# Layers 0 and 1 prepared two tiles ahead of the recurrent layer, a reordered start, and one order for the late iterations

## The reference

```python
# L0: per-sample scaled product, L1: tanh RNN, L2: per-sample rank-8 update of a base matrix, L3: LSTM
x = x + einsum('bsi,io->bso', x * ys[:, None, :], W0) * d[:, None, :]      # ys, d from cond
x = x + scan(h -> tanh(h @ Wh1 + (x_t @ Wx1 + b1)))                         # h0 = cond
x = x + x + x @ (base + A_b @ B_b)       # A_b, B_b = gelu(layernorm(cond) @ w1 + b1) @ w2 + b2
x = x + scan((h, c) -> LSTM(x_t @ Wx3 + b3 + h @ Wh3))                      # h0 = cond, c0 = 0
```

## Time and profile before

| what | value |
|---|---|
| time, median of 3 runs | 1170.16 us (1169.96 to 1170.26) |
| the profiled execution's own time | 1170.03 us |
| its span in the profile | 1168.2 us |
| TensorE busy | 1130.0 us, 97% of the span, 23548 matmuls |
| VectorE busy | 896.1 us, 77% |
| ScalarE busy | 424.4 us, 36% |
| mean granted TensorE clock | 0.994 of full speed |

### The profile page before, as it was taken

One profiled execution on the slowest core, in us unless ns is written; L12 is line 12 of the kernel. 1 busy time (PEld: TensorE's weight loads), 2 busy tenths in 40 slices (PEclk: granted clock), 3 DMA queues, 4 the chain that ended last, 5 costly groups with the idle time before them and its releaser, 6 DMA issues.

```text
span 1168.2 us, 52112 instructions
## 1 busy us (share of the span) xinstructions
PE 1130.0 (97%) x23548; PEld 773.1 (66%) x23548; DVE 896.1 (77%) x2656; ACT 424.4 (36%) x1036; POOL 53.5 (5%) x75
## 2 busy tenths in 40 slices
PE   5779999999999999999999999999999999999997
PEld 3446766776676677667667766766776676677586
DVE  7798777777777777787777778777777877777665
ACT  6784333333333333333333333333333333333322
POOL 0000100000000000000000000000000000000000
PEclk9989999999999999999999999999999999999999
DMA  9991000000000000000000000000000000000000
GB/s 339 404 349 29 21 21 21 3 21 21 21 20 21 21 3 21 21 21 21 20 21 4 21 20 21 21 21 21 3 21 20 21 21 20 12 3 12 12 13 21
DMA packets 24590, 51.08 MB, mean 44 GB/s; under 512 B 4160, under 2 KB 4288, under 8 KB 23344
## 3 DMA queue, kind: packets, MB, share of 16 engines
q1 hardware_dynamic: 24080, 47.56, 11.5%
q10 hardware_dynamic: 288, 0.20, 0.1%
HBM read 39.36 MB, written 8.39 MB: 41 GB/s over the span
## 4 chain that ended last, share of the span: by engine, by line
PE 92%; DMA 4%; SPq 2%; DVE 1%; ACT 1%; issue 0%; DVEq 0%; ACTq 0%
PE ps_gates L1488 55%; PE ps_l L1424 14%; PE ps_x L1424 7%; PE ps_rnn L1534 6%; PE ps_rnn L1537 4%; DMA ring<-in_hw 2%; PE ps_lr L1424 2%; PE ps_z L1424 2%; PE ps_l L1488 1%; DMA big<-in_hw 1%; SPq L395 1%; PE ps_gates L1394 1%; SPq L427 1%; DVE gates_ring L1086 0%; ACT rows L515 0%
## 5 line engine op out<-in xcount | busy, mean ns | idle before, releaser
L1488 PE MATMUL ps_gates<-big,lstm_h 128*32 128x512 f16 (+1 forms) x6144 | 345.0, 373 | 2.5 <-DVE lstm_h L1118 2.5
L1488 PE MATMUL ps_gates<-big,rows 128*32 128x512 f16 (+1 forms) x6144 | 342.8, 372 | 0.6 <-ACT rows L515 0.6
L1488 PEld LDWEIGHTS ps_gates<-big,rows 128*32 128x32 f16 x6144 | 164.6, 97 | 157.1 <-issue 0.7
L1488 PEld LDWEIGHTS ps_gates<-big,lstm_h 128*32 128x32 f16 x6144 | 157.5, 97 | 151.6 <-DVE lstm_h L1118 4.4
L651 ACT ACTIVATE gates_ring<-gates_ring 128x256 f32<-128x256 f32 x128 | 53.4, 417 | 341.7 <-DVE gates_ring L1086 341.7
L1086 DVE SCALAR_TENSOR_TENSOR gates_ring<-ps_gates,tile_un,rows 128x256 f32<-128x256 f32 x248 | 108.7, 478 | 74.3 <-PE ps_gates L1488 72.0
L1534 PE MATMUL ps_rnn<-rnn_h,wh_hi 128*128 128x64 f16 x2048 | 120.6, 192 | 1.9 <-DVE rnn_h L920 1.9
L1537 PE MATMUL ps_rnn<-rnn_h,wh_lo 128*128 128x32 f16 x2048 | 116.4, 177 | 0.0
L1534 PEld LDWEIGHTS ps_rnn<-rnn_h,wh_hi 128*128 128x128 f16 x2048 | 93.1, 97 | 34.5 <-issue 28.8
L1115 DVE SCALAR_TENSOR_TENSOR late<-gates_ring,tile_g,cell_tanh 128x128 f16<-128x128 f32 x128 | 45.0, 352 | 60.7 <-ACT cell_tanh L660 60.7
L1537 PEld LDWEIGHTS ps_rnn<-rnn_h,wh_lo 128*128 128x128 f16 x2048 | 91.2, 97 | 0.0
(11 more groups left out here) (199 smaller groups left out, 1595.7 us busy)
## 6 DMA issues: line engine op xcount, KB each, us to landing
ring<-in_hw SPq DMA_DIRECT2D x16, 1024.0 KB, 15.2
xT_sb<-in_xT SPq DMA_DIRECT2D x32, 256.0 KB, 2.9
outT<-late SPq DMA_DIRECT2D x32, 256.0 KB, 2.0
big<-in_wx SPq DMA_DIRECT2D x5, 1024.0 KB, 14.6
big<-in_wh SPq DMA_DIRECT2D x5, 1024.0 KB, 15.5
big<-in_w SPq DMA_DIRECT2D x1, 1024.0 KB, 6.7
big<-in_hw SPq DMA_DIRECT2D x1, 1024.0 KB, 12.9
late<-in_base SPq DMA_DIRECT2D x1, 1024.0 KB, 14.7
```

The source lines that it names most:

```text
L1488: last = nc.tensor.matmul(by_chunk_of_gate(bank[B * j:B * j + B, columns]), of_step, tile_columns(w, j)[:, gates], start=start, stop=stop, ...
```

## The change

It has four parts. (1) `l0` and `l1` run two tiles ahead of the RNN (`LEAD` = 2, so the loop does tile i + 2): `x1T` gets 3 buffers, `xw1T` 2, and `l0(3)` and `l1(3)` stand in the start. The input tile is loaded, measured and scaled one iteration earlier too; `xs(3)` and `xs(4)` move from POOL to VectorE. (2) In the start the order is new: `rnn(0)` ahead of `l0(1)` and `l0(2)`, `l1(1)` after `rnn(1)`, `l1(2)` ahead of `w2_unit(8)`, `w2_unit(10)` ahead of `rnn(6)`; VectorE and ScalarE follow, with `x1(2)` ahead of `base_diagonal`. (3) The layer norm of the condition waits for its own row alone, and for the other two rows (now `ld_ln`) only later; its square root stands ahead of the squares of `w0`. (4) Iterations 30 and 31, which have no `l0` and `l1` any more, are a loop of their own with the LSTM first; the x2 of tile 31 and L2 of tile 31 move one LSTM step back.

```diff
-        x1T = [sb(f"x1T{q}", [P, KC, STEPS, B]) for q in range(2)]
-        xw1T = sb("xw1T", [P, KC, STEPS, B])
+        x1T = [sb(f"x1T{q}", [P, KC, STEPS, B]) for q in range(X1_RING)]
+        xw1T = [sb(f"xw1T{q}", [P, KC, STEPS, B]) for q in range(LEAD)]
...
         def in_l0(i):
-            return i + 1 < TILES
+            return i + LEAD < TILES
...
# VectorE, the start (SP: load_x(4) and load_x(5) now ahead of and behind b3, waiting for x1_ready)
-            dve.wait_ge(ld_rows, 48)
+            dve.wait_ge(ld_rows, 16)
...
             wh1_low(0)
+            x1_low(0)
+            wh1_low(1)
             x_magnitude(1, 1)
...
             rnn_sums(2)
+            x1(2)
             base_diagonal()
             wx3_low(2, 0)
             rnn_out(2)
             a_magnitude()
-            xs_low(2)
+            xs_low(3)
             rnn_sums(3)
...
             x2(0)
+            x1_low(2)
             xw1(1)
             rnn_sums(4)
-            x1(2)
+            x1(3)
             a_low()
             rnn_out(4)
             x2_low(0)
             wx3_low(2, 1)
-            x1_low(2)
             wx3_low(3, 0)
             rnn_sums(5)
             wx3_low(3, 1)
+            xw1(2)
             rnn_out(5)
+            x1_low(3)
             base_low(0)
...
# VectorE, the new late loop, i = 30 and 31
+            for i in range(TILES - LEAD, TILES):
+                lstm_gates(t)
+                lstm_out(t)
+                rnn_sums(r)
+                rnn_out(r)
+                mask_z(a1)
+                zm_low(a1)
+                lstm_gates(t + 1)
+                lstm_out(t + 1)
+                rnn_sums(r + 1)
+                gate_scales(i)
+                rnn_out(r + 1)
+                lstm_gates(t + 2)
+                lstm_out(t + 2)
+                x3_first(a1)
+                rnn_sums(r + 2)
+                x3_low(a1)
+                lstm_sums(t + 3)
+                rnn_out(r + 2)
+                lstm_cell(t + 3)
+                lstm_turned(t + 3)
+                lstm_out(t + 3)
+                rnn_sums(r + 3)
...
# TensorE, the start
             l1(0)
-            l0(1)
             rnn(0)
+            l0(1)
+            l0(2)
             w2_unit(4)
             rnn(1)
+            l1(1)
             w2_unit(5)
             w2_unit(6)
             rnn(2)
             w2_unit(7)
-            l1(1)
             turn_a()
             rnn(3)
-            l0(2)
+            l0(3)
             rnn(4)
+            l1(2)
             w2_unit(8)
             rnn(5)
             w2_unit(9)
+            w2_unit(10)
             rnn(6)
-            w2_unit(10)
             z(0)
             w2_unit(11)
             rnn(7)
-            l1(2, (0, 1))
+            l1(3, (0, 1))
...
# TensorE, the new late loop
+            for i in range(TILES - LEAD, TILES):
+                lstm(t)
+                rnn(r)
+                z(a1)
+                x3_base(a1, (0, 1))
+                lstm(t + 1)
+                rnn(r + 1)
+                gates_x(t + 2)
+                gates_x(t + 3)
+                lstm(t + 2)
+                rnn(r + 2)
+                x3_base(a1, (2, 3))
+                x3_low_rank(a1)
+                lstm(t + 3)
+                rnn(r + 3)
+                gates_x(t + 4)
```

More of the change, by code:

```diff
@@ L720, in _ @@
             rnn(2)
+            x1_high(2)
             base_squares()
@@ L756, in _ @@
             x2_high(1)
-            xs_high(LAG + 1)
-            for i in range(LAG, TILES):
-                a1, c, t, r = i - LAG + 1, i + 1, STEPS * (i - LAG), STEPS * i
+            xs_high(LAG + LEAD)
+            for i in range(LAG, TILES - LEAD):
+                a1, c, t, r = i - LAG + 1, i + LEAD, STEPS * (i - LAG), STEPS * i
                 lstm_acts(t)
@@ L1218, in _ @@
             xw1(0)
-            tile_undo(1, XT_RING - 1, 1)
+            xs_low(1)
+            xs(2)
+            rnn_sums(0)
             x1(1)
-            rnn_sums(0)
+            xs_low(2)
+            xs(3)
             wx3_scale()
@@ L1274, in _ @@
             gate_scales(0)
+            x_magnitude(LAG + LEAD, 0)
             x3_first(0)
@@ L1327, in _ @@
                 x3_low(a1)
+                rnn_sums(r + 3)
                 if in_l0(i):
[L1329 removed]
                     xw1(c)
[L1331 to L1338 removed]
+                rnn_out(r + 3)
+                lstm_gates(t + 3)
                 lstm_out(t + 3)
@@ L1616, in _ @@
                 x3_base(a1, (0, 1))
-                if in_l0(i):
-                    rnn(r + 1)
-                    lstm(t + 1)
-                else:
-                    lstm(t + 1)
-                    rnn(r + 1)
+                rnn(r + 1)
+                lstm(t + 1)
                 gates_x(t + 2)
@@ L1631, in _ @@
                     l1(c)
-                    rnn(r + 3)
-                    lstm(t + 3)
-                else:
-                    lstm(t + 3)
-                    rnn(r + 3)
+                rnn(r + 3)
+                lstm(t + 3)
+                gates_x(t + 4)
+                if in_rnn(i + 1):
+                    gates_x(t + 5)
+            for i in range(TILES - LEAD, TILES):
+                a1, t, r = i - LAG + 1, STEPS * (i - LAG), STEPS * i
+                lstm(t)
+                rnn(r)
+                z(a1)
+                x3_base(a1, (0, 1))
+                lstm(t + 1)
+                rnn(r + 1)
+                gates_x(t + 2)
+                gates_x(t + 3)
+                lstm(t + 2)
+                rnn(r + 2)
+                x3_base(a1, (2, 3))
+                x3_low_rank(a1)
+                lstm(t + 3)
+                rnn(r + 3)
                 gates_x(t + 4)
```

168 lines of the change are left out of this document (84 added, 84 removed).

## The result

The changed kernel takes 1172.06 us in the median of 20 runs (1169.89 to 1176.77), the kernel before 1170.12 us beside it (20 runs, 1169.96 to 1170.54). The ratio of the means is 1.0021, with a 95% interval of 1.0014 to 1.0028 (that of the medians is 1.0017): slower by a fifth of a percent, at the line of 0.2% that the prediction drew between "same" and "slower". The forecast was 1171.3 with a range of 1167.0 to 1173.6. The ratios further down are those of the means too.

The account below looks back on a forecast made before the run. TensorE, busy 97%, bounds the kernel, with DMA and a nearly slackless VectorE limiting the start. 1170.0 - 1.9 (iterations 30 and 31) + 3.2 (start: 1.5 VectorE, 1.7 cold clock) = 1171.3 us, range 1167.0 to 1173.6.

Parts of the forecast that it names:

- The limits of before: Start of the kernel before: two clocks, DMA and VectorE; VectorE busy 31.12 of 32.80 us, almost no slack.
- VectorE's term in the start, +1.5: Start: magnitude and gates_x(0) come 0.9 + 1.3 - 0.7 = 1.5 us late through VectorE's work.
- The walk of TensorE: Start: TensorE's new order stepped through with earlier durations; rnn(2) ends at 53.0 us, against 51.2 before.
- One cold stretch in the start, +1.7: Start, at l0(1) or l0(2): the clock falls once to half for 3.4 us, costing 1.7 us.
- The loop, 0: Iterations 2 to 29: same order one tile further on, no change; at most 0.2 us shows in iteration 2.
- The end, 0: End of the kernel: steps only change places, z and L2 of tile 31 one step later; 0 us.
- Iteration 30 at 31.5, iteration 31 at 29.3: Late iterations: 30 gains 2.5 us from 34.04, 31 loses 0.6 from 28.73; together -1.9 us.
- The idle of 1.8 ahead of `rnn(r + 3)`: Iterations 30 and 31: TensorE idles 1.8 us because rnn_out(r + 2) stands behind lstm_sums(t + 3) on VectorE.
- The second rival: VectorE isn't the start's limit and the late rnn(r + 3) wait is hidden: 1164.6 to 1166.1, half-case 1168.1; chance 0.15.
- part 4: Iterations 30 and 31: 5.36 us of L0 and L1 leave, LSTM latency gives some back; together -1.9 us.
- the first rival: Start: the clock stays up, so the start ends only 1.5 us late; 1169.6 us, chance 0.28.
- the third rival: Start: the w2 ring slips, unit 15 lands later, lateness of 4.5 to 5.5 stays; 1172.6 to 1173.6, chance 0.21.

Follow-up runs that it names:

- Kernel seven: The kernel before with three parts of VectorE's and ScalarE's wh3 work moved behind the last rows of w2, nothing else: 1170.53 us, ratio 1.0002.
- kernel three: The changed kernel with products nobody reads in four TensorE waits of the start, ahead of rnn(0), l0(2), rnn(3) and rnn(6): 1172.41 us, ratio 1.0019.
- kernel one: The changed kernel with VectorE taking rnn_out(r+2) ahead of lstm_sums(t+3) in iterations 30 and 31: 1172.48 us, ratio 1.0015.
- kernel four: The changed kernel with iteration 30 run RNN first, as before, and only iteration 31 LSTM first: 1174.16 us, ratio 1.0035.
- ten: The changed kernel with three wh3 parts moved behind w2's last rows on VectorE and ScalarE, no filler: 1176.75 us, ratio 1.0046.
- kernels five: The changed kernel with rnn_out(r+2) ahead of lstm_sums(t+3) and products nobody reads in TensorE's longer waits: 1168.80 us, ratio 0.9989.
- six: The changed kernel with rnn_out(r+2) first, longer TensorE waits filled and three wh3 parts moved behind w2's last rows: 1168.07 us, ratio 0.9983.
- eleven: The changed kernel with rnn_out(r+2) first, waits filled, wh3 parts moved, and 6 more unread products ahead of rnn(7): 1168.21 us, ratio 0.9985.

## Why the prediction was right, and where not

The median lies 0.8 us from the forecast and inside the range, and part of that is luck. By its terms the profiled execution should be 1.3 us slower than before; it is 3.0 us slower, 1.7 of them a stretch that the sum doesn't have; the rest agrees because a start 0.5 us better than forecast stands against 0.24 and 0.25 us that were taken as nothing. And the same kernel on another chip had a median of 1174.63, above the range. What held is the mechanism of the start, of VectorE and of the late waits; what the sum lacked is the clock in the late part.

**The limits of before.** Right. Kernel seven shows it: 1.29 us off VectorE and no gain.

**VectorE's term in the start, +1.5.** Right in size: 1.7 us without the clock (kernel three). Its parts: with the clock up `base_diagonal` starts at 55.67 (kernel three), 1.07 us late, where I had 0.9; of the 1.3 us of added pieces and 0.7 us of absorbed waits the magnitude shows 0.6 more.

**The walk of TensorE.** `l0(1)` 36.9 forecast, 37.01 measured; `l0(2)` 41.8 and 42.80; unit 4's end 46.5 and 47.5; `rnn(2)`'s end 53.0 and 54.1. Of the missing microsecond 0.8 is the stretch that I had put between 37 and 46 (`l0(2)` is at 42.02 with the clock up, kernel three).

**One cold stretch in the start, +1.7.** Right that the clock falls here (at 35 in one profile, at 43 in the other of this kernel), wrong in count and effect. The profile has three ahead of 80 us, and together they add 1.0 us (96.98 against 96.0). The one between 35.1 and 38.5 puts `l0(2)` off by 0.78 (42.80 against 42.02 in kernel three) and `rnn_sums(2)` by as much (54.15 against 53.37); the later two add the other 0.2. In two other profiles with three they add 1.4 and 1.8, in one with a single stretch 0.5.

**The loop, 0.** 0.24 us, in iteration 2. I had allowed at most 0.2 there for VectorE's three more operations and left it out of the sum.

**The end, 0.** 0.25 us longer from `lstm(120)` on. No experiment bears on it; why is open.

**Iteration 30 at 31.5, iteration 31 at 29.3.** Right at full clock: 31.74 and 29.19. In the profile of the changed kernel itself iteration 30 is 33.43, with the stretch in it. The idle of 1.8 ahead of `rnn(r + 3)` is 1.72, released by what I said. The second rival's alternative, `rnn_out(r + 2)` in time, was priced at 29.7; kernel one gives 30.96, since 0.93 us of the wait stay.

**The step that failed: part 4 has no clock in it.** I priced what a gap does to the clock in the start, and then wrote down two new idle times of 1.8 us in the tail, as long as the 2.02 and 1.61 us of the earlier trace rows, and gave them only their own length. There nothing covers a stretch: 1.7 us behind either of them, seen at 1083 (the changed kernel, kernel three) and at 1114 to 1120 (kernels four and ten). In the same way I had the magnitude 1.5 us late and didn't ask how long TensorE would then wait ahead of `move_b`: 2.07 us instead of 0.96, and the stretch behind it is exposed again (kernel three). The sum without any exposed stretch is 1170.0 + 1.7 + 0.24 - 2.30 + 0.46 + 0.25 = 1170.4, which is the group of eight runs at 1169.9 to 1170.9, the first rival's case. Each exposed stretch adds 1.7 us to this, and the covered ones some of theirs. The groups' means, 1170.5, 1171.9, 1173.0 and 1175.9, lie 1.4, 1.1 and 2.9 us apart, so a group isn't simply one stretch more.

**The forecast's single number** lies between two groups: 1171.3 is met by few runs. The range to 1173.6 leaves out the six runs at 1175 and 1176. At 1.7 us each those need two or more exposed stretches, or a stretch that holds up TensorE and VectorE together, which none of my cases had. No execution of the changed kernel in that group was profiled; the nearest is kernel four's at 1175.47, 3.6 us of it in the start and 1.7 in iteration 31. So what the upper group is made of is worked out, not shown. As for the ring, the third rival puts its times down to it, and in no profile of the changed kernel or of those made from it did TensorE wait for a transfer behind 73 us.

The Trainium skill, "TensorE: Matmul & The Clock Gate", What's actually happening, says of a kernel's first products that how many of them run slowly differs from run to run of one kernel. The runs agree, and for waits inside a kernel too: the same instructions had their first stretch at 35 us in one execution of the changed kernel and at 43 in the other, and one in iteration 30 in one of them only. I had read the page for whether the clock would fall, and should have read from it that one kernel can have several times.

## What to carry to other kernels

Price each new wait of TensorE twice: its own length, and, if waits like it are followed by a fall of the clock in the profiles at hand (here some of 1.71 us and more), the half-clock stretch behind it, at the chance with which it occurs and at full price where no other engine covers it. A change that trades work for waits can leave the best run where it was and raise the median. If a wait can't be removed, products that nobody reads hold the clock at no cost that shows (kernels five, six and eleven: medians of 1168.1 to 1168.8 us, nine or ten of 11 runs within 1.6 us; their lower best runs come from the other edits in them), and they are the quickest way to find out what a kernel is worth at full clock. Compare distributions, with the granted clock beside each run, not medians of a few.
